# Cross-attention and a routed feed-forward layer on one core: VectorE's LayerNorm and routing steps put at the end of each group of heads

## The chip, the cores and the metric

The kernel runs on one core of one Trainium2 chip. The metric is the device time of one execution in microseconds (us). Five engines work side by side, each through its own list of instructions in order: TensorE (PE, matmuls), VectorE (DVE), ScalarE (ACT), GpSimd (POOL) and SyncE (SP, which issues DMAs). They meet at semaphores only.

## The reference

```python
x = x + xattn(layernorm(x), ctx, Wq, Wk, Wv, Wo, bo)     # x: 16 x 256 x 128, ctx: 16 x 1601 x 96, 16 heads of 64
x = x + ffn(layernorm(x), router_weight, ...)             # 32 experts, 4 groups of 8, top 2 groups, top 4 experts
...
def _route(tokens, router_weight, router_bias):
    scores = sigmoid(tokens @ router_weight.T)
    sfc = scores + router_bias
    group_scores = top_k(sfc.reshape(T, 4, 8), 2)[0].sum(-1)
    gmask = the 2 best groups of 4
    topk_idx = top_k(where(gmask > 0, sfc, 0), 4)
    topk_w = scores[topk_idx]; topk_w = topk_w / (topk_w.sum(-1) + 1e-20) * 2.5
```

## The kernel before, in words

All 16 batches are worked through one after the other. A batch has 256 queries and 1601 keys, its 16 heads go in four groups of four heads, so there are 64 groups, called here by their number i = 0 to 3 in the batch. The loop on each engine covers two batches (`par` 0 and 1) a turn, eight turns in all.

In a group the 1601 keys go in 13 steps s = 0 to 12 of up to 128 keys (the last has 65). A step is: TensorE makes the scores in PSUM (`scores`, 6 matmuls of 512 columns, since each fp32 product is made from a high and a low fp32r half); ScalarE takes the exponential twice (`exp`), once as fp32 `p_full`, once as its high half `p_hi`; the low half `p_lo` = `p_full` - `p_hi` is a subtraction over 128 x 1024, made by GpSimd for steps 3, 5, 7 and 9 (`POOL_STEPS`) and by VectorE for the nine others (`lo(s)`, L1004); TensorE then weighs the values (`weigh`, 6 matmuls), two steps behind the scores.

Between these, TensorE does side jobs, whose results land in two banks of PSUM (`side`), used in turn, and which VectorE has to empty: TensorE waits in `side_jobs` until the job before the last has been emptied (`s_drain`). The table `PLACES` says which jobs stand at which step t, and all engines go through it in the same order. M jobs (32 a group) make scores for the next group's maxima, and VectorE takes the maximum (L1016); Y jobs project finished heads and VectorE adds them to the tokens `x1`; T turns the maxima; the two Q jobs at step 12 project queries of a later group. L turns normalised tokens for the attention of the next batch, N turns those of a finished batch for the feed-forward part, R makes router logits.

VectorE also has steps that are no jobs. LayerNorm is `token_stats` (means and variances, ending in `var_eps`), a power -0.5 on GpSimd (`deviations`), and `normalise` (`xn`). Routing is a chain of small dependent instructions on 128 x 64 values and less. Before, the function `between` puts these inside the group, by step t: the statistics after `lo(6)` at t = 7 of groups i = 0 and 1, `normalise` at t = 3 of groups 1 and 2, and in group 3 the routing in four parts at t = 6, 7, 8 and 10.

GpSimd, besides its four `p_lo` a group, splits a quarter of the next batch's context into halves at each group (`split_piece`, four instructions, L368 to L373). After the 64 groups comes the feed-forward part: 8 chunks of 512 tokens, 17 pairs of experts (the first the shared one) in each, and there VectorE also routes the last tokens in the second chunk.

Of the kernel before, what the change touches and what calls it, by code (L numbers as in the profile page):

```python
# [11 lines left out]
P = 128  # L12
# [6 lines left out]
def xattn_moe(nc, x, ctx_keys, ctx_turned, attn_w, bo, router_wT, router_b, moe_w, out):  # L19
# [29 lines left out]
    with stack:  # L49
# [9 lines left out]
        w_all = sb(stack, "w_all", [P, T + 2, 2 * E])  # L59
# [7 lines left out]
        power = sb(stack, "power", [P, 2])  # L67
        stats = sb(stack, "stats", [P, 2, 6])
        moments = sb(stack, "moments", [P, 2, 2])
        var_eps = sb(stack, "var_eps", [P, 2])  # L70
        rstd = sb(stack, "rstd", [P, 2])
        xn = sb(stack, "xn", [P, 2, D])
# [126 lines left out]
        PLACES = {2: ("MM", "M"), 3: ("MM", "M"), 4: ("MM", "MM"), 5: ("MM", "MX"), 6: ("MM", "MM"),  # L199
                  7: ("MM", "MM"), 8: ("MM", "MY"), 9: ("MM", "MM"), 10: ("MM", "MM"), 11: ("YY", "YT"),  # L200
                  12: ("", "QQ")}
        EXTRA = ("", "L", "N", "R")
        KINDS = "MLNRYTQ"

        def places(i):
            return {t: tuple(part.replace("X", EXTRA[i]) for part in ab) for t, ab in PLACES.items()}

# [91 lines left out]
        def _(pool):  # L299
# [7 lines left out]
            def deviations(count):  # L307
                pool.wait_ge(s_var, count)
                pool.tensor_tensor(rstd[:, :], var_eps[:, :], power[:, :], ALU.pow).then_inc(s_rstd, 1)
# [12 lines left out]
            deviations(1)  # L322
# [3 lines left out]
            pool.memset(v_lo[:, :, :, DC:OW].bitcast(F32), 0.0)  # L326
            pool.memset(choice[:, :, E:E + TOP_K], -BIG)
# [30 lines left out]
            def split_piece(bb, par, i):  # L358
# [10 lines left out]
                pool.tensor_copy(v_hi[:, other, tiles, 0:DC], keys_nat[:, tiles, :]).then_inc(s_sh, 1)  # L369
                pool.wait_ge(s_sh, bb * (2 * NGB) + (g + 2))  # L370
# [5 lines left out]
            with pool.Fori(0, B // 2) as bb:  # L376
                for par in range(2):
                    for i in range(NGB):
                        g = group_of(par, i)
                        split_piece(bb, par, i)  # L380
# [4 lines left out]
                        if i < 2:  # L385
                            deviations(bb * 4 + (2 * par + 2 + i))

            deviations(2 * B + 2)
# [19 lines left out]
        def _(pe):  # L408
# [3 lines left out]
            def turn_tokens(where, count):  # L412
                pe.wait_ge(s_xn, count)
                for t in range(2):
                    mm = pe.transpose(where[:, t * P:(t + 1) * P], xn[:, t, :], ident[:, :])
                mm.then_inc(s_fill, 1)
# [38 lines left out]
            turn_tokens(bank(J0_X), 1)  # L455
# [73 lines left out]
            def body(bb, par, i):  # L529
# [7 lines left out]
                def side_jobs(kinds):  # L537
                    for kind in kinds:
# [5 lines left out]
                        if kind == "M":  # L544
                            if k == 0:
                                pe.wait_ge(s_qh, bb * (4 * NGB) + (2 * g + 4))
                            if i == NGB - 1 and k in (0, 3 * NM // 4):
                                pe.wait_ge(s_v, bb * (2 * NGB) + (par * NGB + (2 * NGB - 1 if k == 0 else 2 * NGB)))
                            max_scores(where, k, (i + 1) % 2, next_par).then_inc(s_fill, 1)
                        elif kind == "L":  # L550
                            turn_tokens(where, bb * 4 + (2 * par + 2))
                        elif kind == "N":
                            turn_tokens(where, bb * 4 + (2 * par + 3))
# [28 lines left out]
                pe.wait_ge(s_ex, n + S)  # L582
                scores(0, (i + 1) % 2, next_par)
# [21 lines left out]
            turn_tokens(bank(JOBS_END + GH), 2 * B + 2)  # L605
# [10 lines left out]
            def turn_routing(c):  # L616
                for t in range(4):
                    mm = pe.transpose(op[0:2 * E, 1, t * P:(t + 1) * P], w_all[:, 2 + c * 4 + t, :], ident[:, :])
                mm.then_inc(s_wf, 1)
# [18 lines left out]
            for c in range(NCH):  # L638
                for q in range(NP):
# [25 lines left out]
                    if q == 10 and c + 1 < NCH:  # L665
                        if c:
                            pe.wait_ge(s_fin, c)
                        if c + 1 == NCH - 1:
                            pe.wait_ge(s_rw, B + 1)
# [6 lines left out]
        def _(act):  # L676
# [52 lines left out]
            def body(bb, par, i):  # L729
# [20 lines left out]
                for s in range(1, S):  # L750
                    exp(s)
                    if s == 5 and EXTRA[i]:
                        j = job_at[i][EXTRA[i]][0]
                        where, filled = bank(jobs0 + j), jobs + (j + 1)
                        if EXTRA[i] == "L":
                            tokens_hi(where, 1 - par, filled)
                        elif EXTRA[i] == "N":
# [76 lines left out]
        def _(dve):  # L834
# [11 lines left out]
            def token_stats(tiles, base=0):  # L846
                for q in range(2):
                    ins = dve.bn_stats(stats[:, q, :], x1[:, tiles[q], :])
                link(ins, base)
                carry()  # L850
                for q in range(2):
                    ins = dve.bn_aggr(moments[:, q, :], stats[:, q, :])
                link(ins, base)
                dve.tensor_scalar(var_eps[:, :], moments[:, :, 1], EPS, None, ALU.add).then_inc(s_var, 1)

            def normalise(tiles, count):
                dve.wait_ge(s_rstd, count)
                for q in range(2):
                    ins = dve.tensor_scalar(xn[:, q, :], x1[:, tiles[q], :], moments[:, q, 0:1], rstd[:, q:q + 1],  # L859
# [39 lines left out]
            def add_one(count):  # L899
                dve.wait_ge(s_ls, count)  # L900
                dve.tensor_scalar(ra[:, :, :], ex[:, :, :], 1.0, None, ALU.add).then_inc(s_drain, 1)

            def route_scores(drained, base=0):
                dve.wait_ge(s_drain, drained)
# [8 lines left out]
                link(ins, base)  # L913

            def route_groups(base=0):
                flat = g_sum[:, :, :].rearrange("p t g -> p (t g)")
                link(dve.tensor_tensor(flat, top8[:, :, 0], top8[:, :, 1], ALU.add), base)  # L917
# [9 lines left out]

            def route_experts(base=0):
                for t in range(2):
                    kept = choice[:, t, 0:E].rearrange("p (g e) -> p g e", g=N_EGROUP)  # L930
                    keep = g_keep[:, t, :].rearrange("p (g a) -> p g a", a=1).to_broadcast([P, N_EGROUP, E // N_EGROUP])
                    ins = dve.tensor_tensor(kept, kept, keep, ALU.mult)
                link(ins, base)
# [3 lines left out]
                link(ins, base)  # L937
                carry()
# [6 lines left out]

# [224 lines left out]
```

## Time and profile before

| | us |
|---|---|
| median of 3 runs (lowest to highest) | 3604.51 (3602.98 to 3604.76) |
| the profiled execution | 3602.96 |
| its span, first to last instruction | 3600.8 |
| 64 groups, from the first output kept to the last | 43.1 to 3263.8 |
| TensorE busy | 3386.3 (94%) |
| VectorE busy | 2578.8 (72%) |
| ScalarE busy | 1935.5 (54%) |
| GpSimd busy | 1076.8 (30%) |
| mean granted clock of TensorE | 0.975 of full |

Each engine's share is of the span. The records of matmuls overlap: each lasts longer than the distance to the next one, so an engine may be called busy and still not be at its fastest. The row on idle time, in square brackets behind an instruction, tells how long its engine had done nothing and whose result ended that.

### The profile page before, as it was taken

The numbers are of one execution on the slowest core, as the hardware profiler recorded it, in microseconds if no ns is written. First come the engines' busy times: TensorE is split into PE (matmuls) and PEld (weight loads), VectorE is DVE, ScalarE is ACT, GpSimd is POOL, SyncE is SP. The second block draws the span as 40 slices with busy tenths as digits, with TensorE's granted clock in tenths as the row PEclk, the third lists the DMA queues.
The fourth block names the chain that finished last, engine by engine and source line by source line (L and its number), as shares of the span: only waits on it lengthen the run. The fifth ranks groups of instructions, "written<-read, shape, count | busy, mean of one in ns | idle before, by whom it ended". The sixth has DMA issues, their size and how long they took to land.

```text
span 3600.8 us, 50491 instructions
## 1 busy us (share of the span) xinstructions
PE 3386.3 (94%) x15589; PEld 2655.2 (74%) x15589; DVE 2578.8 (72%) x4960; ACT 1935.5 (54%) x2239; POOL 1076.8 (30%) x737
## 2 busy tenths in 40 slices
PE   7999999999999999999999999999999999999999
PEld 6777777777777777777777777777777777777887
DVE  6777777777777777777777777777777777776655
ACT  4555555555555555555555555555555555555554
POOL 4222232222222222222222222222232222324555
PEclk9999999999999999999999999999999999999999
DMA  2000000000000000000000000000000000000000
GB/s 84 1 15 1 16 1 15 1 15 2 2 14 1 16 1 15 1 15 2 15 1 1 16 1 15 1 15 2 15 1 1 16 1 15 1 15 27 9 7 9
DMA packets 8682, 35.98 MB, mean 10 GB/s; under 512 B 1657, under 2 KB 2306, under 8 KB 8130
## 3 DMA queue, kind: packets, MB, share of 16 engines
q1 hardware_dynamic: 8386, 32.29, 2.9%
q8 instruction: 154, 2.52, 0.3%
q14 instruction: 142, 1.16, 0.1%
HBM read 29.92 MB, written 2.10 MB: 9 GB/s over the span
## 4 chain that ended last, share of the span: by engine, by line
PE 77%; DVE 11%; issue 9%; POOL 1%; DVEq 0%; ACT 0%; POOLq 0%; DMA 0%; ACTq 0%
PE side L449 10%; PE op L513 9%; PE op L516 9%; PE st L499 9%; PE op L519 9%; PE st L502 9%; PE st L505 9%; PE side L525 3%; DVE m_part L1016 3%; DVE p_lo L1004 3%; PE st L614 2%; PE st L612 2%; PE st L613 2%; DVE xn L859 1%; DVE g_sum L917 1%
## 5 line engine op out<-in xcount | busy, mean ns | idle before, releaser
L742 ACT ACTIVATE p_full<-st 128x1024 f32<-128x1024 f32 (+1 forms) x832 | 855.0, 1028 | 1457.2 <-PE st L505 1457.2
L1016 DVE TENSOR_REDUCE m_part<-side 128x1 f32<-128x402 f32 x2048 | 1096.7, 571 | 529.9 <-PE side L449 520.6
L383 POOL TENSOR_TENSOR p_lo<-p_full,p_hi 128x1024 fp32r<-128x1024 f32 x256 | 649.1, 2536 | 2096.8 <-ACT p_hi L745 2096.8
L1004 DVE TENSOR_TENSOR p_lo<-p_full,p_hi 128x1024 fp32r<-128x1024 f32 (+1 forms) x576 | 709.0, 1231 | 266.3 <-ACT p_hi L745 266.3
L745 ACT ACTIVATE p_hi<-st 128x1024 fp32r<-128x1024 f32 (+1 forms) x832 | 850.6, 1022 | 0.0
L449 PE MATMUL side<-cT_hi,qT_hi 96*128 96x402 f32 x2048 | 613.1, 364 | 178.5 <-DVE m_part L1016 165.0
L449 PEld LDWEIGHTS side<-cT_hi,qT_hi 96*128 96x128 f32 x2048 | 395.0, 193 | 344.6 <-DVE m_part L1016 220.2
L499 PE MATMUL st<-qT_hi,cT_hi 97*128 97x512 f32 (+1 forms) x1668 | 548.3, 410 | 3.2 <-DMA qT_hi<-m_row 3.0
L513 PE MATMUL op<-p_hi,v_hi 128*97 128x512 f32 (+1 forms) x1664 | 540.4, 407 | 0.0
L516 PE MATMUL op<-p_lo,v_hi 128*97 128x512 f32 (+1 forms) x1664 | 533.0, 402 | 0.0
L519 PE MATMUL op<-p_hi,v_lo 128*97 128x512 f32 (+1 forms) x1664 | 532.3, 402 | 0.0
L502 PE MATMUL st<-qT_lo,cT_hi 96*128 96x512 f32 (+1 forms) x1668 | 529.5, 398 | 0.0
L505 PE MATMUL st<-qT_hi,cT_lo 96*128 96x512 f32 (+1 forms) x1668 | 523.4, 395 | 0.0
L502 PEld LDWEIGHTS st<-qT_lo,cT_hi 96*128 96x128 f32 (+1 forms) x1668 | 312.9, 188 | 82.9
L505 PEld LDWEIGHTS st<-qT_hi,cT_lo 96*128 96x128 f32 (+1 forms) x1668 | 306.8, 184 | 83.8
L516 PEld LDWEIGHTS op<-p_lo,v_hi 128*97 128x97 f32 (+1 forms) x1664 | 277.4, 167 | 120.2
L519 PEld LDWEIGHTS op<-p_hi,v_lo 128*97 128x97 f32 (+1 forms) x1664 | 277.4, 167 | 119.7
L499 PEld LDWEIGHTS st<-qT_hi,cT_hi 97*128 97x128 f32 (+1 forms) x1668 | 301.2, 189 | 32.5 <-issue 3.7
L513 PEld LDWEIGHTS op<-p_hi,v_hi 128*97 128x97 f32 (+1 forms) x1664 | 273.3, 168 | 30.9
L402 POOL TENSOR_TENSOR h_lo<-hid,h_hi 128x512 fp32r<-128x512 f32 x136 | 176.2, 1295 | 137.1 <-ACT h_hi L807 137.0
L525 PEld LDWEIGHTS side<-B_all,oT 97*128 97x128 f32 x1040 | 153.7, 200 | 28.8 <-DVE m_part L1016 12.2
L892 DVE SCALAR_TENSOR_TENSOR x<-side,recip,x 128x128 f32 (+1 forms) x520 | 158.5, 347 | 11.1 <-DVE recip L889 2.5
(142 smaller groups left out, 2760.9 us busy)
## 6 DMA issues: line engine op xcount, KB each, us to landing
keys_nat<-in_ctx_keys SPq DMA_DIRECT2D x18, 624.0 KB, 5.8
keys_tur<-in_ctx_turned SPq DMA_DIRECT2D x18, 603.0 KB, 5.0
out_x<-x SPq DMA_DIRECT2D x8, 256.0 KB, 2.0
x<-in_x SPq DMA_DIRECT2D x1, 1920.0 KB, 12.8
w_rest<-in_moe_w SPq DMA_DIRECT2D x1, 1152.0 KB, 6.8
qT_hi<-m_row SPq DMA_DIRECT2D x65, 4.0 KB
w_first<-in_moe_w SPq DMA_DIRECT2D x1, 960.0 KB, 5.0
aw<-in_attn_w SPq DMA_DIRECT2D x2, 448.0 KB, 6.1
```

The costliest lines, as they stand in the source:

```text
L383: pool.tensor_tensor(p_lo[:, slot(s), :], p_full[:, s % 2, :], p_hi[:, slot(s), :].bitcast(F32), ALU.subtract).then_inc(s_lo_pool, 1)
L449: return pe.matmul(where[:, 0:MAXW], qT_hi[0:DC, slot, tile * P:(tile + 1) * P], cT_hi[0:DC, par, part * MAXW:(part + 1) * MAXW], start=Tr ...
L499: pe.matmul(st[0:m, s % 2, j, :], cT_hi[:, par, keys], qT_hi[:, slot, halves[j]], start=True, stop=False)
L502: pe.matmul(st[0:m, s % 2, j, :], cT_hi[0:DC, par, keys], qT_lo[:, slot, halves[j]], start=False, stop=False)
L505: mm = pe.matmul(st[0:m, s % 2, j, :], cT_lo[:, par, keys], qT_hi[0:DC, slot, halves[j]], start=False, stop=True)
L513: pe.matmul(op[0:OW, j, :], v_hi[0:m, par, s, :], p_hi[0:m, slot(s), halves[j]], start=(s == 0), stop=False)
L516: pe.matmul(op[0:OW, j, :], v_hi[0:m, par, s, :], p_lo[0:m, slot(s), halves[j]], start=False, stop=False)
L519: mm = pe.matmul(op[0:OW, j, :], v_lo[0:m, par, s, :], p_hi[0:m, slot(s), halves[j]], start=False, stop=(s == S - 1))
L742: act.activation(p_full[0:m, s % 2, :], both(st[0:m, s % 2]), ACT.Exp, scale=SCALE)
L745: act.activation(p_hi[0:m, slot(s), :], both(st[0:m, s % 2]), ACT.Exp, scale=SCALE).then_inc(s_ex, 1)
L1004: dve.tensor_tensor(p_lo[0:m, slot(s), :], p_full[0:m, s % 2, :], p_hi[0:m, slot(s), :].bitcast(F32), ALU.subtract).then_inc(s_lo, 1)
L1016: dve.tensor_reduce(m_part[:, at:at + 1], where[:, 0:MAXW], AX.X, ALU.max).then_inc(s_drain, 1)
```

## The change

The function `between` is taken out, and a function `after_jobs` is called behind the last side job of the group instead. The statistics of all four tiles of tokens (two for the next batch, two finished) are taken in one go at the end of group 0; `normalise` for all four and the middle part of the routing stand at the end of group 1; the last part of the routing at the end of group 2; its first part at the end of group 3. L moves from group 1 to group 2 and N one step on, to t = 6. In group 3 the R job's bank is now given free by a memset (`exponentials_seen`), and the addition of one goes with the first part of the routing. The small tiles of LayerNorm double, so that four tiles fit. On GpSimd one power instruction over four columns at step 3 of group 1 takes the place of two over two columns, at the ends of groups 0 and 1.

```diff
-                def between(t):
...
-                    if i == 0 and t == 7:
-                        token_stats([dve.snap(bb * 4 + (2 * par + 4 + q)) for q in range(2)], links)
-                    elif i == 1 and t == 3:
-                        normalise([dve.snap(bb * 4 + (2 * par + 4 + q)) for q in range(2)], bb * 4 + (2 * par + 2))
...
-                    elif i == 3 and t == 6:
-                        route_scores(jobs + (job_at[i]["R"][0] + 1), links)
-                    elif i == 3 and t == 7:
+                def after_jobs():
...
+                    if i in (0, 1):
+                        tiles = [dve.snap(bb * 4 + (2 * par + q)) for q in (4, 5, 0, 1)]
+                    if i == 0:
+                        dve.wait_ge(s_drain, jobs + (job_at[i]["Y"][-1] + 1))
+                        token_stats(tiles, 0, links)
+                    elif i == 1:
+                        normalise(tiles, 0, bb * 2 + (par + 2))
                         route_groups(links)
...
+                    elif i == 2:
                         route_weights(bass.ds(bb * 4 + 2 * par, 2), links)
+                    else:
+                        route_scores(links)
...
-                    between(t)
                     side_jobs(at[t][1])
-
...
+                after_jobs()
...
-        EXTRA = ("", "L", "N", "R")
+        EXTRA = {2: {5: "L", 6: "N"}, 3: {5: "R"}}
...
-            def split_piece(bb, par, i):
+            def piece_hi(bb, par, i):
...
+            def piece_lo(bb, par, i):
...
-                        split_piece(bb, par, i)
+                        piece_hi(bb, par, i)
+                        piece_lo(bb, par, i)
...
-                        if i < 2:
-                            deviations(bb * 4 + (2 * par + 2 + i))
-
+                            if s == 3 and i == 1:
+                                deviations(bb * 2 + (par + 2), slice(0, 4))
...
                     if c == 1:
-                        if q == 8:
-                            route_scores(JOBS_END + GH + 2)
+                        if q == 5:
+                            route_groups()
+                        elif q == 8:
+                            route_weights(slice(T, T + 2))
                         elif q == 10:
+                            route_scores()
+                        elif q == 12:
                             route_groups()
-                        elif q == 12:
-                            route_experts()
                         elif q == 14:
-                            route_weights(slice(T, T + 2))
+                            route_weights(slice(T + 2, T + 4))
```

TensorE's wait for the context before the maxima of the next batch now counts the high half only (`s_sh`), and a wait for all of it (`s_v`) stands ahead of the first scores of that batch.

VectorE's order before, in group 3 at steps t = 6 and 7; `m_part` rows are M jobs, and each of them gives TensorE a bank back:

```order
L1016 TENSOR_REDUCE m_part<-side 128x1
L1003 REGISTER_ALU
L1004 TENSOR_TENSOR p_lo<-p_full,p_hi 128x1024
L917 TENSOR_TENSOR g_sum<-top8 128x8
L840 REGISTER_ALU
L920 TENSOR_TENSOR g_more<-g_sum 128x32
L921 TENSOR_TENSOR g_same<-g_sum 128x32
L840 REGISTER_ALU
L923 TENSOR_TENSOR g_same<-g_same,earlier 128x32
```

VectorE's order in the changed kernel, from the last side jobs of group 1 (the two `qT_lo`) on into group 2:

```order
L888 TENSOR_TENSOR qT_lo<-side,qT_hi 96x512
L870 ISA
L872 TENSOR_SCALAR xn<-x1,moments,rstd 128x128 x4
L933 TENSOR_TENSOR g_more<-g_sum 128x32
L934 TENSOR_TENSOR g_same<-g_sum 128x32
L852 REGISTER_ALU
L936 TENSOR_TENSOR g_same<-g_same,earlier 128x32
L852 REGISTER_ALU
L937 TENSOR_TENSOR g_more<-g_more,g_same 128x32
```

The comparison of groups (`g_more`, `g_same`) stood behind a `p_lo` and ahead of M jobs in the middle of group 3; now it stands between the last Q job of group 1 and the `p_lo` of step 0 of group 2, together with four `xn`.

GpSimd's order in the changed kernel, where group 0 ends and group 1 goes to its step 3:

```order
L392 TENSOR_TENSOR p_lo<-p_full,p_hi 128x1024
L371 CAST cT_hi<-keys_tur 96x402
L372 CAST v_hi<-keys_nat 128x4x96
L378 REGISTER_ALU
L379 TENSOR_TENSOR cT_lo<-keys_tur,cT_hi 96x402
L381 TENSOR_TENSOR v_lo<-keys_nat,v_hi 128x4x96
L391 REGISTER_ALU
L392 TENSOR_TENSOR p_lo<-p_full,p_hi 128x1024
L308 ISA
L309 TENSOR_TENSOR rstd<-var_eps,power 128x4
```

The four instructions of the split stand as before behind the last `p_lo` of one group and ahead of the first `p_lo` of the next; only the power instruction has moved.

## Rows read from the trace of the kernel before

**Rows 1.** The page: busy time and share of each engine; the chain by engine.
```profile
PE 3386.3 (94%) x15589; PEld 2655.2 (74%) x15589; DVE 2578.8 (72%) x4960; ACT 1935.5 (54%) x2239; POOL 1076.8 (30%) x737
...
PE 77%; DVE 11%; issue 9%; POOL 1%; DVEq 0%; ACT 0%; POOLq 0%; DMA 0%; ACTq 0%
```

**Rows 2.** One line, L727 (one a group): count, ns min/median/max, first and last start.
```profile
L727 ACT ACTIVATE oT<-op x65: 1024/1028/1028, 43.1 to 3263.8; 97x1024 f32<-97x1024 f32 x65
```

**Rows 3.** Stretches, groups i = 0 to 3 of one batch: length, busy us (instructions), PEclk, DMA.
```profile
1049.03:1097.22 48.19, 46.28 (x218) 36.14 (x217) 34.62 (x63) 27.08 (x31) 16.90 (x14) 1.00 0.00 1
1097.22:1148.72 51.50, 47.83 (x220) 37.33 (x219) 36.73 (x66) 27.47 (x32) 13.62 (x9) 0.97 0.00 1
1148.72:1196.74 48.02, 46.02 (x220) 36.35 (x219) 34.57 (x60) 27.47 (x31) 12.99 (x8) 1.00 0.09 27
1196.74:1250.82 54.08, 50.03 (x224) 38.72 (x223) 40.70 (x97) 27.32 (x31) 10.12 (x4) 0.94 0.01 2
```

**Rows 4.** TensorE in order of time: start, us, instruction, count, idle before.
```profile
1106.04 0.35 PE L449 MATMUL side<-cT_hi,qT_hi 96*128 96x402 f32 x1
1108.38 0.45 PE L449 MATMUL side<-cT_hi,qT_hi 96*128 96x402 f32 x1 [2.00 <-DVE m_part L1016]
...
1120.68 0.53 PE L449 MATMUL side<-cT_hi,qT_hi 96*128 96x402 f32 x2
...
1124.29 1.19 PE L449 MATMUL side<-cT_hi,qT_hi 96*128 96x402 f32 x2 [1.67 <-DVE m_part L1016]
...
1224.27 1.19 PE L449 MATMUL side<-cT_hi,qT_hi 96*128 96x402 f32 x2 [2.95 <-DVE m_part L1016]
```

**Rows 5.** VectorE in order of time, the `normalise` of group 1.
```profile
1105.19 2.65 DVE L859 TENSOR_SCALAR xn<-x,moments,rstd 128x128 f32 x2
```

**Rows 6.** GpSimd in order of time, its first `p_lo` of the same group.
```profile
1104.99 2.51 POOL L383 TENSOR_TENSOR p_lo<-p_full,p_hi 128x1024 fp32r<-128x1024 f32 x1 [18.31 <-ACT p_hi L745]
```

**Rows 7.** Four lines of VectorE: count, ns min/median/max, first and last start.
```profile
L859 DVE TENSOR_SCALAR xn<-x,moments,rstd x68: 334/1616/2880, 5.3 to 3271.2; 128x128 f32 x64, 128x128 f32<-128x128 f32 x4
...
L854 DVE TENSOR_SCALAR var_eps<-moments x34: 169/1537/1544, 3.8 to 3269.9; 128x2 f32<-128x2 f32 x34
...
L917 DVE TENSOR_TENSOR g_sum<-top x17: 433/2349/2354, 213.1 to 3340.2; 128x8 f32<-128x8 f32 x17
...
L901 DVE TENSOR_SCALAR ra<-ex x17: 195/1881/1890, 205.1 to 3275.6; 128x64 f32<-128x64 f32 x17
```

**Rows 8.** Stretches at the lower clock, in groups 1 and 3 of that batch.
```profile
1124.20:1127.60 3.40, 3.31 (x8) 2.34 (x9) 1.58 (x4) 0.47 (x1) 0.00 (x0) 0.50 0.00 0
...
1223.20:1230.00 6.80, 5.73 (x16) 4.46 (x17) 4.67 (x22) 0.17 (x1) 0.00 (x0) 0.50 0.00 0
```

**Rows 9.** VectorE in order of time, where group 1 ends and group 2 begins.
```profile
1144.41 1.28 DVE L875 TENSOR_TENSOR qT_lo<-side,qT_hi 96x512 fp32r<-96x512 f32 x2
1148.87 1.23 DVE L1004 TENSOR_TENSOR p_lo<-p_full,p_hi 128x1024 fp32r<-128x1024 f32 x1 [3.18 <-ACT p_hi L745]
```

**Rows 10.** TensorE in order of time, the first values weighed in group 2.
```profile
1151.20 0.63 PE L513 MATMUL op<-p_hi,v_hi 128*97 128x512 f32 x2
```

**Rows 11.** VectorE in order of time: statistics, middle of the routing, end of the routing.
```profile
1121.42 0.48 DVE L848 BATCH_NORM_STATS2 stats<-x 128x6 f32 x2
...
1222.34 0.19 DVE L920 TENSOR_TENSOR g_more<-g_sum 128x32 f32<-128x32 f32 x1
...
1223.63 1.06 DVE L1016 TENSOR_REDUCE m_part<-side 128x1 f32<-128x402 f32 x2
...
1235.77 0.21 DVE L947 TENSOR_TENSOR ra<-struck,choice 128x64 f32<-128x64 f32 x1
...
1237.66 0.23 DVE L956 TENSOR_TENSOR w_all<-ra,w_all 128x64 f32 x1
```

**Rows 12.** Stretches of 39.5 us in the feed-forward part: the third chunk, the second.
```profile
3372.73:3412.27 39.54, 39.54 (x179) 32.54 (x178) 23.43 (x36) 20.61 (x38) 23.29 (x19) 1.00 0.02 8
3333.20:3372.70 39.50, 38.01 (x169) 30.55 (x168) 30.78 (x71) 19.39 (x34) 22.14 (x18) 1.00 0.01 2
```

More of the change, by code:

```diff
@@ L66, in xattn_moe @@
         earlier = sb(stack, "earlier", [P, N_EGROUP, N_EGROUP])
[L67 to L72, printed above, removed]
+        power = sb(stack, "power", [P, 4])
+        stats = sb(stack, "stats", [P, 4, 6])
+        moments = sb(stack, "moments", [P, 4, 2])
+        var_eps = sb(stack, "var_eps", [P, 4])
+        rstd = sb(stack, "rstd", [P, 4])
+        xn = sb(stack, "xn", [P, 4, D])
         x2f = sb(stack, "x2f", [P, 2 * P])
@@ L305, in link, with deviations @@
                 pool.wait_ge(s_plink, steps[0])
-            def deviations(count):
+            def deviations(count, which):
                 pool.wait_ge(s_var, count)
-                pool.tensor_tensor(rstd[:, :], var_eps[:, :], power[:, :], ALU.pow).then_inc(s_rstd, 1)
+                pool.tensor_tensor(rstd[:, which], var_eps[:, which], power[:, which], ALU.pow).then_inc(s_rstd, 1)
             link(pool.memset(ident[:, :], 0.0))
@@ L326, in _ @@
             pool.memset(v_lo[:, :, :, DC:OW].bitcast(F32), 0.0)
+            pool.memset(sigmoid[:, :, :], 0.0)
+            pool.memset(g_sum[:, :, :], 0.0)
+            pool.memset(choice[:, :, 0:E], 0.0)
             pool.memset(choice[:, :, E:E + TOP_K], -BIG)
@@ L369, in split_piece @@
                 pool.tensor_copy(v_hi[:, other, tiles, 0:DC], keys_nat[:, tiles, :]).then_inc(s_sh, 1)
+            def piece_lo(bb, par, i):
+                g, other = group_of(par, i), 1 - par
+                cols = slice(i * MAXW, (i + 1) * MAXW)
+                tiles = slice(PIECES[i], PIECES[i] + 4)
                 pool.wait_ge(s_sh, bb * (2 * NGB) + (g + 2))
@@ L582, in body @@
                 pe.wait_ge(s_ex, n + S)
+                if i == NGB - 1:
+                    pe.wait_ge(s_v, bb * (2 * NGB) + (par * NGB + 2 * NGB))
                 scores(0, (i + 1) % 2, next_par)
@@ L844, in carry, with token_stats, normalise @@
                 dve.memset(spare[:, :], 0.0)
-            def token_stats(tiles, base=0):
-                for q in range(2):
-                    ins = dve.bn_stats(stats[:, q, :], x1[:, tiles[q], :])
+            def token_stats(tiles, first, base=0):
+                for q, tile in enumerate(tiles):
+                    ins = dve.bn_stats(stats[:, first + q, :], x1[:, tile, :])
                 link(ins, base)
                 carry()
-                for q in range(2):
-                    ins = dve.bn_aggr(moments[:, q, :], stats[:, q, :])
+                for q in range(len(tiles)):
+                    ins = dve.bn_aggr(moments[:, first + q, :], stats[:, first + q, :])
                 link(ins, base)
-                dve.tensor_scalar(var_eps[:, :], moments[:, :, 1], EPS, None, ALU.add).then_inc(s_var, 1)
-            def normalise(tiles, count):
+                which = slice(first, first + len(tiles))
+                dve.tensor_scalar(var_eps[:, which], moments[:, which, 1], EPS, None, ALU.add).then_inc(s_var, 1)
+            def normalise(tiles, first, count):
                 dve.wait_ge(s_rstd, count)
-                for q in range(2):
-                    ins = dve.tensor_scalar(xn[:, q, :], x1[:, tiles[q], :], moments[:, q, 0:1], rstd[:, q:q + 1],
+                for q, tile in enumerate(tiles, first):
+                    ins = dve.tensor_scalar(xn[:, q, :], x1[:, tile, :], moments[:, q, 0:1], rstd[:, q:q + 1],
                                             ALU.subtract, ALU.mult)
@@ L926, in route_groups @@
                 link(dve.tensor_scalar(g_keep[:, :, :], g_keep[:, :, :], TOPK_EGROUP - 0.5, None, ALU.is_lt), base)
[L928 to L933, printed above, removed]
+                kept = choice[:, :, 0:E].rearrange("p t (g e) -> p t g e", g=N_EGROUP)
+                keep = g_keep[:, :, :].rearrange("p t (g a) -> p t g a", a=1)
+                link(dve.tensor_tensor(kept, kept, keep.to_broadcast([P, 2, N_EGROUP, E // N_EGROUP]), ALU.mult), base)
                 carry()
@@ L937, in route_experts, with route_weights @@
                 link(ins, base)
+            def route_weights(tiles, base=0):
                 carry()
@@ L944, in route_experts @@
                 link(ins, base)
-            def route_weights(tiles, base=0):
                 link(dve.tensor_tensor(ra[:, :, :], struck[:, :, 0:E], choice[:, :, 0:E], ALU.not_equal), base)
```

68 lines of the change are left out of this document (31 added, 37 removed).

## The prediction

> **What bounds the kernel now.** I read the page first: TensorE is busy for 94% of the span, and the chain that ended last lies on it for 77%, but also for 11% on VectorE and for 9% on "issue" [rows 1]. So there are places where TensorE stands and VectorE is late. To find them I cut the span into the 64 groups. The copy of the output (L727) runs once a group, 65 times from 43.1 to 3263.8 us, which is 50.32 us a group, 201.3 us a batch [rows 2]. The view by stretches then shows that the four groups of a batch are unlike: 48.19, 51.50, 48.02 and 54.08 us, though TensorE has nearly the same work (218, 220, 220, 224 matmuls in the records). The two long ones also have a lower mean clock, 0.97 and 0.94 [rows 3].
>
> TensorE in order of time shows the stalls. In group 1 an M job starts at 1106.04 and the next at 1108.38, where two M jobs that meet no wait start 0.18 us apart (0.53 for a pair of 0.35 each). That is 2.16 us lost, and what ended it was VectorE's maximum. It happens again at 1124.29, and in group 3 at 1224.27 with 2.95 us of idle time [rows 4]. The maxima are late because of what stands ahead of them on VectorE: the two `xn` at 1105.19 took 2.65 us together [rows 5]. One `xn` takes 0.334 us at its quickest, 1.616 in the median; `var_eps`, on two columns, 0.169 and 1.537; `g_sum`, on eight columns, 0.433 and 2.349; the addition of one, 0.195 and 1.881 [rows 7]. A duration that doesn't go with the size is a wait inside the instruction. GpSimd's `p_lo` ran from 1104.99 for 2.51 us, to 1107.50 [rows 5, 6], and the first `xn` began 0.2 us after it and the pair was over 0.34 us after it: VectorE was held until GpSimd was done. The Trainium skill, GPSIMD Engine Reference, "Key points", says that GpSimd shares its SBUF interfaces with VectorE and contends with instructions of two SBUF inputs or in a mode that uses both ports; the trace agrees for these four, and the M jobs' maxima, read from PSUM, come right behind without such a wait.
>
> The clock is the second part. It is at 0.50 for 3.4 us behind the second stall of group 1 and for 6.8 us behind the long one of group 3 [rows 8]. Both times it fell while or just after TensorE stood; in the third chunk of the feed-forward part TensorE is busy for all of 39.54 us and the clock is at 1.00 [rows 12].
>
> **The change, part by part.**
>
> *Stalls removed.* With no LayerNorm or routing step ahead of M jobs, the stalls go. Group 0 loses that of `var_eps`, group 1 those of `xn` and `var_eps`, group 2 that of `xn`: each 2.16 to 2.3 us with the late restart, I take 2.2, so 4 x 2.2 = 8.8 us a batch. Group 3 loses the long one, 2.95 us idle plus 0.17 (a record is 0.35 long and the next could start 0.18 after it) plus a slow pair (1.19 for 0.53, of which half is the clock): 3.4 us. The added one costs VectorE 1.881 - 0.195 = 1.7 us more than it need; what reaches TensorE lies between 0 and 1.7, I take 1.0. The chain of `route_weights` took 2.12 us from 1235.77 to 1237.89 [rows 11] ahead of M jobs; between 0 and 2.1 reaches TensorE, I take 0.5 as an estimate. Sum 13.7 us a batch.
>
> *Clock.* In the two slow stretches TensorE was busy for 3.31 and 5.73 us [rows 8]; at full clock the same work takes half, so 1.65 + 2.85 = 4.5 us a batch. By the Trainium skill, TensorE: Matmul & The Clock Gate, "Terms", the penalty is about the throttled time by one less the ratio of clocks; from the 10.2 us that would be 5.1 us, and the forecast 10 us lower. I stay with the busy time, as part of the slow stretch was idle anyway.
>
> *Cross-check.* 13.7 + 4.5 = 18.2 us a batch. The other way: group 2 has one stall and no clock loss, 48.02 - 2.2 = 45.8; group 0 gives 48.19 - 2.2 = 46.0 [rows 3]. Four such groups are 183.4, against 201.3: 17.9 us. I take 18.1, and 16 batches give 290 us. VectorE is then busy for about 33 us of 45.8, so it does not become the bound.
>
> *What is put at the ends.* Between the last Q job (VectorE done at 1145.69) and the `p_lo` of the next group's step 0 (1148.87, it waits for the exponential) VectorE is idle for 3.18 us. That `p_lo` is over at 1150.10 and TensorE first needs it at 1151.20 [rows 9, 10], so a further 1.1 us of lateness costs nothing: a cover of 4.28 us. Prices without the hold: the pair of statistics is 0.48 us [rows 11], the aggregates I estimate at no more, `var_eps` at 0.17 [rows 7], so 1.1 for two tiles and up to 2.1 us for four. End of group 1: four `xn` at up to 0.334, 1.3 us, the comparisons from 1222.34 to 1223.63, 1.3 us [rows 7, 11], and the selection, three instructions estimated at 0.2 each like the small rows: 3.0 to 3.3 us. End of group 2: five more of that kind, overlapping, 0.6 (an estimate), and the 2.12 of the weights: 2.7. End of group 3: addition, reciprocal, bias, eight small maxima and a sum, by the same 0.2 each with the maxima overlapping about 2.2, at most 3 (an estimate too). All lie below 4.28, three at or below 3.0. They are cheap there only if GpSimd is idle; ahead of its first `p_lo` in group 1 it had been idle for 18.31 us [rows 6], that is since 1086.68, over the whole end of group 0 (1097.22). I take 0 for the four ends; bounds 0 and 1 us each.
>
> *L and N in one group, the power on GpSimd, TensorE's waits.* L is no longer in group 1, and stands with N in group 2: the same matmuls. `xn` is ready a whole group earlier than it is read. One GpSimd power instruction a batch goes. The wait for `s_v` is long met. Cost 0, cover: several steps of 3.5 us. The split on GpSimd is not moved at all (its order shows it), so that part of the change is nothing.
>
> *Feed-forward part.* In the second chunk VectorE routes twice instead of once, beside a GpSimd that works all the time, so holds come back. Before, this chunk's stretch had 1.5 us of TensorE idle in 39.50 [rows 12]. VectorE was busy there for 30.78 us against 23.43, so the routing took 7.4 us of busy time; it takes nearly twice that now, in bigger pieces. Between +1 and +9 us, I take +5.
>
> *Sum.* Against the profiled execution's span: 3600.8 - 290 + 5 = 3315.8. The median of the runs lies 3.7 above the span (3604.51): 3319.5 us, 7.9% less.
>
> **Rivals.**
>
> *The clock falls as before.* If the low clock had another cause than the stalls, 4.5 x 16 = 72 us stay: 3391 us. For it: stalls in groups 0 and 2 are followed by no drop, both have a mean clock of 1.00 [rows 3]. Against it: both drops come right behind a stall [rows 4, 8], and the unbroken chunk has none [rows 12]. Chance 7%.
>
> *The ends spill, or new stalls take part of the gain.* The small steps have waits of a few hundredths each that could be longer after a register instruction, or N's and L's copies hold a bank in group 2. At 0.5 to 1 us an end that is 32 to 64 us: 3350 to 3383 us. For it: group 1's end fills the idle time. Against: the further 1.1 us. Chance 13%.
>
> *Slower than before.* GpSimd works at the group ends after all, and every held instruction there waits for it: place, the end of each group ahead of `p_lo` of step 0; price 2.2 us for each held one. With four an end, 8.8 + 2.4 - 4.28 = 6.9 us are lost at each, 27.6 a batch against 18.1 won: 3604 + 152 = 3756 us. It decides once the ends take 8.8 us on the mean. Against it is the 18.31 us of idle time. Chance 3%.
>
> *The gain is not there* (M jobs wait for something else right behind, and the groups stay near 50 us): 3590 to 3610 us. Against: group 2 has 2.0 us without a matmul in all, which is its one stall [rows 3, 4]. Chance 2%.
>
> **The numbers.** 75% for the forecast with its own range, 3303 to 3345. The range must leave out no more than 2 in 10: from 3303 to 3375 it takes in most of the spill. A difference of 0.2%, 7 us, is about what a measurement of this kernel can tell. Faster by more than that 0.95, within it 0.02, slower 0.03.
>
> **What the profile after would show.** Right: all four groups of a batch 45.5 to 46.2 us long, clock 1.00 from group 0 to 63, `xn`, `var_eps`, `ra` and `g_sum` in the loop at their shortest durations, VectorE's idle time ahead of `p_lo` of step 0 down from 3.18 to 0.1 to 1.6 us, TensorE's waits for `m_part` near nothing, the second feed-forward chunk some us longer. Wrong: low clock still once or twice a batch, long small instructions at the ends, TensorE waiting ahead of the first `op` matmuls of a group, or groups that differ by over 1 us.

## The result, and the profile after

| | before | after |
|---|---|---|
| median of the runs, us | 3603.94 (3602.98 to 3604.76) | 3340.26 (3337.08 to 3342.82) |
| the profiled execution, span | 3600.8 | 3335.1 |
| 64 groups, first output kept to the last | 43.1 to 3263.8 | 41.3 to 2992.7 |
| mean granted clock | 0.975 | 0.996 |

The ratio is 0.9268 with a 95% interval of 0.9252 to 0.9284: 264 us, or 7.3%, less, where 285 were forecast (3319 us). In the spans the 64 groups went from 3220.7 to 2951.4 us, 269.3 less, the part behind them from 337.0 to 342.4, 5.4 more, and the part ahead from 43.1 to 41.3. This last part took between 41.2 and 47.1 us in the twelve profiles of this case, and not by kernel (the changed one had 41.3 and 41.2, a variant that differs only behind it 45.8). So a difference of up to 5 us between two medians need not come from the groups, and for small differences the time of the 64 groups is the better measure: the changed kernel's two profiles have 2951.4 and 2952.2 us.

The page of the changed kernel, busy time and the chain that ended last:

```profile
PE 3285.0 (98%) x15589; PEld 2611.9 (78%) x15589; DVE 2414.3 (72%) x4954; ACT 1937.9 (58%) x2239; POOL 1073.8 (32%) x724
...
PE 89%; issue 6%; DVE 3%; POOL 2%; ACT 0%; DMA 0%; DVEq 0%; POOLq 0%; ACTq 0%
```

VectorE's share of the chain fell from 11% to 3% [rows 1], and its busy time by 164 us, though it does nearly the same work (4954 instructions for 4960): that was time held inside instructions. Four groups of one batch of the changed kernel by stretches, as in [rows 3], and below them group 0 of another batch, the third:

```profile
965.25:1011.23 45.98, 45.75 (x219) 36.16 (x218) 33.80 (x67) 27.10 (x31) 16.35 (x13) 1.00 0.00 1
1011.23:1056.70 45.47, 45.47 (x219) 36.24 (x218) 34.15 (x71) 27.10 (x30) 14.00 (x9) 1.00 0.01 1
1056.70:1103.35 46.65, 46.16 (x223) 36.54 (x222) 34.56 (x75) 27.88 (x33) 13.03 (x8) 1.00 0.10 28
1103.35:1149.36 46.01, 46.01 (x223) 36.72 (x222) 33.42 (x71) 27.33 (x32) 10.14 (x4) 1.00 0.01 2
409.32:458.44 49.12, 47.26 (x219) 37.16 (x218) 33.80 (x67) 27.22 (x30) 17.03 (x13) 0.97 0.01 2
```

The groups are nearly alike now, close to the length worked out, but for two things to explain: group 2 is 0.6 to 1.2 us longer than the others, and one group 0 took 49.12 us with the clock at 0.97. The small instructions of VectorE, lines as in [rows 7]:

```profile
L872 DVE TENSOR_SCALAR xn<-x,moments,rstd x68: 330/337/2879, 5.4 to 3000.1; 128x128 f32 x64, 128x128 f32<-128x128 f32 x4
...
L867 DVE TENSOR_SCALAR var_eps<-moments x18: 169/170/493, 4.0 to 2998.8; 128x4 f32<-128x4 f32 x16, 128x2 f32<-128x2 f32 x2
...
L928 DVE TENSOR_TENSOR g_sum<-top x17: 171/172/484, 223.9 to 3075.3; 128x8 f32<-128x8 f32 x17
...
L917 DVE TENSOR_SCALAR ra<-ex x17: 178/181/856, 222.1 to 3072.4; 128x64 f32<-128x64 f32 x17
```

Their medians are at the shortest value: 0.337 for 1.616 us, 0.170 for 1.537, 0.172 for 2.349, 0.181 for 1.881. VectorE in order of time over the end of group 1, the place of [rows 9]:

```profile
1052.38 1.28 DVE L888 TENSOR_TENSOR qT_lo<-side,qT_hi 96x512 fp32r<-96x512 f32 x2
1053.58 1.10 DVE L872 TENSOR_SCALAR xn<-x,moments,rstd 128x128 f32 x4
1054.60 0.18 DVE L933 TENSOR_TENSOR g_more<-g_sum 128x32 f32<-128x32 f32 x1
...
1056.17 0.18 DVE L945 MAX8 best<-choice 128x8 f32<-128x32 f32 x1
1056.84 1.23 DVE L1013 TENSOR_TENSOR p_lo<-p_full,p_hi 128x1024 fp32r<-128x1024 f32 x1 [0.49 <-ACT p_hi L756]
```

The work there takes from 1053.66 to 1056.35, 2.7 us, and leaves 0.49 us idle ahead of a `p_lo` that starts 0.14 us after the group's begin, as before.

Two waits of TensorE are new in the changed kernel's list of waits (who waited for whom, us in total, times, longest):

```profile
PE side L424 <- DVE m_part L1025: 7.8, 16, 0.5
...
PE op L522 <- DVE p_lo L1013: 6.8, 7, 1.9
...
PE side L458 <- DVE m_part L1025: 1.7, 8, 0.2
```

The last is the wait that stood at 165 us in the kernel before. The first is N in group 2, once a batch; the second comes ahead of the first values weighed, seven times, that is once for each turn of the loop but the first. The chain of the changed kernel in order of time at one of them (start, us, what; L1070 is VectorE's loop):

```profile
408.02 0.18 DVE g_sum L928
408.20 0.03 issue
408.23 0.04 DVEq L1070
408.27 0.03 issue
408.30 0.06 DVEq L1070
408.36 3.23 issue
411.59 0.06 DVEq L1070
411.65 0.05 issue
411.70 2.05 DVE p_lo L1013
413.75 0.04 issue
413.79 0.71 PE op L522 x2
```

Routing ends, VectorE's loop branches, and 3.23 us pass in which it waits for nothing that the profile shows. Then `p_lo` of step 0 starts 2.38 us late against the group's begin, where 0.14 is usual, and is held by GpSimd's split on top (2.03 for 1.23 us). GpSimd's last two instructions of that split are these:

```profile
411.61 1.04 POOL L379 TENSOR_TENSOR cT_lo<-keys_tur,cT_hi 96x402 fp32r<-96x402 f32 x1
412.61 1.93 POOL L381 TENSOR_TENSOR v_lo<-keys_nat,v_hi 128x384 fp32r<-128x384 f32 x1
```

The two engines take turns. `p_lo` starts while `cT_lo` runs, and needs 0.8 us more than it takes alone; `cT_lo` is over at 412.65. `v_lo` then stands behind `p_lo` and needs 1.0 us more than the 0.93 that it takes alone. TensorE waited 1.86 us here, and its clock fell for 3.4 us right behind. At the six other turns `p_lo` came 2.1 to 2.2 us behind the group's begin, TensorE waited 0.8 to 0.9 us, the clock stayed, and the group took 46.7 to 46.8 us.

In the kernel before such a turn lay inside the 3.2 to 3.7 us of idle time at a group's end, and no `p_lo` of step 0 in the loop was late. The Trainium skill, Runtime: NRT & Kernel Launch, "Instruction fetch mechanics", says that a taken branch to a page out of the current window forces a fetch by DMA before execution goes on; the trace has packets of the instruction queues from 407 to 412.5 us, 6 of them, and none in mid-turn from 961 to 966. The packets are not told apart by engine, and the other engines come round their loops too, so that VectorE's 3.23 us are this fetch is not shown. That they belong to the loop's turn is shown by the runs below.

### The profile page after: what moved, and what is told of

Same layout as the page of the kernel before. It is cut to its first block, busy times and chain, and to the rows that moved or that the text cites. A ratio compares the mean times of both kernels' runs of the same rounds, so it can differ in the third digit from the quotient of the medians.

```text
span 3335.1 us, 50432 instructions
## 1 busy us (share of the span) xinstructions
PE 3285.0 (98%) x15589; PEld 2611.9 (78%) x15589; DVE 2414.3 (72%) x4954; ACT 1937.9 (58%) x2239; POOL 1073.8 (32%) x724
## 4 chain that ended last, share of the span: by engine, by line
PE 89%; issue 6%; DVE 3%; POOL 2%; ACT 0%; DMA 0%; DVEq 0%; POOLq 0%; ACTq 0%
PE st L511 11%; PE st L508 11%; PE op L522 11%; PE st L514 11%; PE op L525 10%; PE side L458 10%; PE op L528 10%; PE side L534 3%; PE st L623 2%; PE st L625 2%; PE st L624 2%; POOL p_lo L392 1%; PE op L623 1%; PE op L625 1%; PE op L624 1%
## 5 line engine op out<-in xcount | busy, mean ns | idle before, releaser
L458 PE MATMUL side<-cT_hi,qT_hi 96*128 96x402 f32 x2048 | 567.0, 347 | 1.8 <-DVE m_part L1025 1.7
L508 PE MATMUL st<-qT_hi,cT_hi 97*128 97x512 f32 (+1 forms) x1668 | 540.5, 405 | 2.9 <-DMA qT_hi<-m_row 2.9
L522 PE MATMUL op<-p_hi,v_hi 128*97 128x512 f32 (+1 forms) x1664 | 527.5, 398 | 6.8 <-DVE p_lo L1013 6.8
L525 PE MATMUL op<-p_lo,v_hi 128*97 128x512 f32 (+1 forms) x1664 | 519.8, 393 | 0.0
L528 PE MATMUL op<-p_hi,v_lo 128*97 128x512 f32 (+1 forms) x1664 | 519.6, 393 | 0.0
L458 PEld LDWEIGHTS side<-cT_hi,qT_hi 96*128 96x128 f32 x2048 | 385.2, 188 | 120.8 <-DVE m_part L1025 7.5
L525 PEld LDWEIGHTS op<-p_lo,v_hi 128*97 128x97 f32 (+1 forms) x1664 | 269.8, 162 | 115.6
L528 PEld LDWEIGHTS op<-p_hi,v_lo 128*97 128x97 f32 (+1 forms) x1664 | 270.0, 162 | 115.1 <-issue 0.2
L522 PEld LDWEIGHTS op<-p_hi,v_hi 128*97 128x97 f32 (+1 forms) x1664 | 265.2, 164 | 38.6 <-DVE p_lo L1013 9.1
L1116 DVE TENSOR_TENSOR gu_mul<-st,act_g 128x512 f32<-128x512 f32 x128 | 88.4, 691 | 102.8 <-PE side L670 95.7
```

Of the source, the lines that this page charges most:

```text
L458: return pe.matmul(where[:, 0:MAXW], qT_hi[0:DC, slot, tile * P:(tile + 1) * P], cT_hi[0:DC, par, part * MAXW:(part + 1) * MAXW], start=Tr ...
L508: pe.matmul(st[0:m, s % 2, j, :], cT_hi[:, par, keys], qT_hi[:, slot, halves[j]], start=True, stop=False)
L522: pe.matmul(op[0:OW, j, :], v_hi[0:m, par, s, :], p_hi[0:m, slot(s), halves[j]], start=(s == 0), stop=False)
L525: pe.matmul(op[0:OW, j, :], v_hi[0:m, par, s, :], p_lo[0:m, slot(s), halves[j]], start=False, stop=False)
L528: mm = pe.matmul(op[0:OW, j, :], v_lo[0:m, par, s, :], p_hi[0:m, slot(s), halves[j]], start=False, stop=(s == S - 1))
```

## The experiments

The kernel before ran beside each of them. Its median was 3606.7 us beside the first four, 3608.26 beside the next four and 3606.12 beside the last two. A line "..." in an edit stands for lines left out.

**LayerNorm half a step later, in the kernel before.**

```diff
-                    if i == 0 and t == 7:
+                    if i == 0 and t == 8:
...
-                    elif i == 1 and t == 3:
+                    elif i == 1 and t == 4:
...
-                    elif i == 1 and t == 7:
+                    elif i == 1 and t == 8:
...
-                    elif i == 2 and t == 3:
+                    elif i == 2 and t == 4:
```

> The kernel before, with only its LayerNorm steps half a step later: the statistics of groups 0 and 1 at t = 8 instead of 7, the two normalise of groups 1 and 2 at t = 4 instead of 3. The same VectorE instructions still stand ahead of M jobs in the middle of the group, but where GpSimd is between two of its p_lo. Theory of the hold (the stalls come from VectorE waiting inside an instruction for GpSimd): each of the four stalls of 2.2 us shrinks to under 0.7, and with the second stall of group 1 its clock loss of 1.65 us goes: 4 x 1.5 to 2.2 and 1.65 are 8 to 10 us a batch, so 3604 - 128 to 160 = 3444 to 3476 us. Rival (any VectorE work ahead of M jobs in mid-group stalls TensorE, whatever GpSimd does): the same stalls at another place, 3595 to 3610 us.

Measured: 3436.33 us, ratio 0.9531 (0.9516 to 0.9546), 170 us less, more than either theory had written down. The 64 groups took 3056.0 us for 3220.7. Its groups of one batch, and two of its lines:

```profile
995.20:1041.16 45.96, 45.76 (x218) 36.15 (x217) 33.18 (x63) 27.09 (x31) 16.91 (x14) 1.00 0.00 1
1041.16:1086.92 45.76, 45.76 (x220) 36.42 (x219) 33.25 (x66) 27.47 (x31) 13.68 (x9) 1.00 0.00 1
1086.92:1132.65 45.73, 45.73 (x221) 36.42 (x220) 32.51 (x60) 27.48 (x32) 13.01 (x8) 1.00 0.10 28
1132.65:1186.78 54.13, 50.09 (x224) 38.77 (x223) 40.70 (x97) 27.31 (x31) 10.12 (x4) 0.94 0.01 2
```

```profile
L859 DVE TENSOR_SCALAR xn<-x,moments,rstd x68: 336/341/2879, 5.3 to 3104.7; 128x128 f32 x64, 128x128 f32<-128x128 f32 x4
...
L854 DVE TENSOR_SCALAR var_eps<-moments x34: 169/169/172, 3.7 to 3103.3; 128x2 f32<-128x2 f32 x34
```

The same instructions, still in mid-group and ahead of M jobs, cost TensorE nothing once they don't meet GpSimd's `p_lo`: groups 0 to 2 stand at 45.7 to 46.0 us. For LayerNorm the hold is shown, and the rival on the amount of work falls. Of the 264 us of the change, about 170 are the meeting of LayerNorm and GpSimd. The rest is group 3, which is untouched here: 54.13 against 46.0 us, less the new costs below. There the rows show the same pattern (`g_sum` 2.349 us in the median before, 0.172 after). But no run moved the routing within group 3 alone, so how much of this part was the hold, and how much the work in that place, is argued and not shown.

**N as the second side job of its place.**

```diff
-        EXTRA = {2: {5: "L", 6: "N"}, 3: {5: "R"}}
+        EXTRA = {2: {3: "N", 5: "L"}, 3: {5: "R"}}
```

> The changed kernel with N of group 2 at t = 3 instead of t = 6, so that it is the second side job in its place and not the third. Theory: the 0.9 us by which group 2's step at N is longer (4.45 against 3.53 us) come from three side jobs on two banks in a row, TensorE waits 0.49 us for the first to be emptied; at t = 3 the wait and its restart go, only N's two transposes (0.2 us) stay: 0.7 us a batch, 11 us, ratio to the changed kernel 0.9967, about 3329 us. Rival (N costs its time wherever it stands, through ScalarE's copy ahead of an exponential): no change, 3340 us.

Measured: 3328.92 us, 11.3 less than the changed kernel's 3340.26; ratio to before 0.9232 (0.9219 to 0.9245). In the profile the wait of N for `m_part` is gone, and group 2 has 45.9 us for 46.65, which is 0.7 us a batch and 11.5 in all. The theory of three jobs on two banks holds.

**Which turn's routing is late.** In these two the condition was written the wrong way round: the kernel labelled as leaving the routing out of the first batch leaves it out of the second, and the other way about. Each expectation belongs to the other's kernel; they are quoted as they stand.

```diff
-                    else:
+                    elif par == 0:
                         route_scores(links)
...
```

> The changed kernel without route_scores at the end of group 3 of the first of the two batches of a loop turn (half of the tokens get wrong routing, the work left out is about 2.2 us of VectorE per turn). Theory of the loop's turn (VectorE needs 3.5 us to come round its loop, and route_scores ahead of it makes the first p_lo late; in mid-turn nothing is late): no change against the changed kernel, 3340 us. Rival (the end of group 3 is too full wherever it stands): 3 to 5 us less.

This kernel keeps the routing at the end of the first batch, in mid-turn, and has none ahead of the branch. Its five runs took 3326.4 to 3332.66 us, the median is 3326.61, ratio 0.9229 (0.9217 to 0.9242), 13.6 less than the changed kernel. The expectation that belongs to it, the one below, had 8 to 9; by the groups of the profile it is 8.6.

> The changed kernel without route_scores at the end of group 3 of the second batch of a loop turn, the one ahead of the branch (half of the tokens get wrong routing). Theory of the loop's turn: 7 turns lose 0.8 us each less, and the one with 2.0 us and a clock drop (3.1 us) too: 8 to 9 us less than the changed kernel, 3331 us. Rival (the end of group 3 is too full wherever it stands): 3 to 5 us less, as without the one of the first batch.

With `elif par == 1:` the routing stays ahead of the branch and is left out in mid-turn. Measured: 3336.73 us, ratio 0.9254 (0.9242 to 0.9267), 3.5 less. The expectation that belongs to it is the one above: no change by the theory, 3 to 5 us less by the rival. So by its time alone this kernel did what the rival said. VectorE in order of time at the same loop top, first of the one without routing ahead of the branch, then of the one with it:

```profile
782.19 1.23 DVE L1013 TENSOR_TENSOR p_lo<-p_full,p_hi 128x1024 fp32r<-128x1024 f32 x1 [3.18 <-ACT p_hi L756]
```

```profile
780.55 0.17 DVE L928 TENSOR_TENSOR g_sum<-top 128x8 f32<-128x8 f32 x1
783.72 1.48 DVE L1013 TENSOR_TENSOR p_lo<-p_full,p_hi 128x1024 fp32r<-128x1024 f32 x1 [3.00 <-issue]
```

In the first the next `p_lo` waits for the exponential, in the second for the branch, 3.00 us. In the profiles the 64 groups took 2942.8 us without routing ahead of the branch and 2947.3 without it in mid-turn, against 2951.4. The first is 8.6 us less, as the theory has it. The second is 4.1 less, and its groups tell where: after a turn group 0 still takes 46.5 to 46.7 us, and in mid-turn `p_lo` of step 0 is as punctual as in the changed kernel, with the routing and without it. What went is the one fall of the clock (49.1 us down to 46.5, 2.6 us), and three of the mid-turn `p_lo` of step 1 missed GpSimd's split (45.5 for 46.0 us, 1.5 together). So the end of group 3 was not too full in mid-turn, and the theory stands.

**The changed kernel again**, as the base of the three that follow.

> The changed kernel again, unedited, as the base of the three others of this call: 3337 to 3343 us.

Measured: 3340.95 us (3337.62 to 3346.33), ratio 0.9264 (0.9251 to 0.9277). Its groups ran from 41.2 to 2993.4, 2952.2 us.

**The first part of the routing at the end of group 0**, behind the statistics. The last batch's part stands behind the loop.

```diff
...
                     if i == 0:
...
                         token_stats(tiles, 0, links)
+                        route_scores(links)
...
-                    else:
-                        route_scores(links)
...
             steps[0] = head_steps + B // 2 * links_per_turn
+            route_scores()
```

> The changed kernel with route_scores at the end of group 0, behind the statistics, instead of the end of group 3; nothing is left out. Theory of the loop's turn (VectorE needs 3.2 to 3.4 us to come round its loop, 2.1 us of routing ahead of the branch make the first p_lo of a turn late): the seven loop tops lose their 0.8 us and the one its 3.1, and the end of group 0, 1.6 and 2.1 us, stays under the cover of 4.28: 9 to 13 us less than the changed kernel, ratio 0.997. Rival (the cost goes with the amount of work at an end, and group 0's end is now the fullest): 16 ends are late instead of 7 or 8, 5 to 15 us more.

Measured: 3332.03 us, 8.9 less than its base; ratio 0.9233 (0.9220 to 0.9246). In the loop TensorE waits for no `p_lo` any more, and the clock stays up. VectorE in order of time over this fullest end:

```profile
1006.61 1.28 DVE L888 TENSOR_TENSOR qT_lo<-side,qT_hi 96x512 fp32r<-96x512 f32 x2
1007.81 0.86 DVE L860 BATCH_NORM_STATS2 stats<-x 128x6 f32 x4
...
1011.09 0.18 DVE L928 TENSOR_TENSOR g_sum<-top 128x8 f32<-128x8 f32 x1
1011.39 1.23 DVE L1013 TENSOR_TENSOR p_lo<-p_full,p_hi 128x1024 fp32r<-128x1024 f32 x1
```

3.4 us of work from 1007.89 to 1011.27 put `p_lo` 0.46 us behind the group's begin for the usual 0.14, and nothing follows from it. The lateness that costs nothing was read as 1.1 us from [rows 9, 10], and the loop's turns of the changed kernel bear it out: there `p_lo` was 2.0 us later than usual and TensorE waited 0.8.

**Both edits together.**

> Both edits, route_scores at the end of group 0 and N at t = 3. If the two costs are apart, they add: 11 us for N and 9 to 13 for the loop's turn, 3340 - 22 = 3318 us, ratio to the changed kernel 0.993 to 0.994. If they hide one another, about 3328.

Measured: 3321.41 us (3316.57 to 3322.39), ratio 0.9204 (0.9192 to 0.9217), 19.5 less than the base. Alone the two edits gave 8.9 and 11.3, 20.2 together, so the two costs add. The 64 groups take 2931.2 us, 45.8 each.

**And GpSimd's split in group 0 behind its `p_lo` of steps 3 and 5.**

```diff
-                        piece_hi(bb, par, i)
-                        piece_lo(bb, par, i)
+                        if i:
+                            piece_hi(bb, par, i)
+                            piece_lo(bb, par, i)
...
+                            if i == 0 and s == 3:
+                                piece_hi(bb, par, i)
+                            if i == 0 and s == 5:
+                                piece_lo(bb, par, i)
```

> The kernel with both edits, and in group 0 GpSimd splits its quarter of the context behind its p_lo of steps 3 (high halves) and 5 (low halves), not at the start of the group. Theory of the hold: the p_lo of step 1 on VectorE, held there to 2.0 us instead of 1.22, is free, and group 0's 0.5 us at its second pair of M jobs go; the high halves (1 us) fit between two of VectorE's p_lo, the low ones (1.9 us) may hold the p_lo of step 6 by up to 1 us, which has more slack than the one of step 1: 4 to 8 us less, about 3311. Rival (the hold only moves): 3315 to 3322, as without the edit.

Measured: 3314.82 us (3310.16 to 3315.5), ratio to before 0.9184 (0.9171 to 0.9196), 6.6 less than without the edit, and all its runs lie below all of those. The profiles' groups went from 2931.2 to 2923.9 us. The `p_lo` of step 1 in group 0, first without and then with the edit:

```profile
961.05 2.01 DVE L1013 TENSOR_TENSOR p_lo<-p_full,p_hi 128x1024 fp32r<-128x1024 f32 x1
```

```profile
964.09 1.21 DVE L1018 TENSOR_TENSOR p_lo<-p_full,p_hi 128x1024 fp32r<-128x1024 f32 x1
```

Over all 576 `p_lo` of VectorE the longest is 1.227 us now, where it was 1.996 in the kernel before. So the hold did not move to another `p_lo`, as the rival had it. This is the best version found, 26 us under the changed kernel.

**A stall put back, without routing or LayerNorm.**

```diff
+                    if i == 1 and t in (7,):
+                        for _ in range(5):
+                            link(dve.memset(xn[:, :, :], 0.0), links)
...
```

> The changed kernel with five extra memsets of 128 x 512 in a row on VectorE (no routing, no LayerNorm, and not held by GpSimd in the kernel before) ahead of M jobs at t = 7 of group 1, about 2.2 us if one takes 0.4 us. Theory of the clock (it falls where TensorE stands too long, not at a place of the program): one stall of about 2 us a batch, 16 x 2 = 32 us; stalls of this size had no drop behind them in groups 0 and 2 before, so the clock stays at 1.00 in most batches: 3365 to 3385 us. Rival (the place in group 1 makes the drop): also 16 drops of 1.6 us, 3400 us.

Measured: 3419.52 us, ratio 0.9480 (0.9464 to 0.9496): 79 us over the changed kernel, more than either theory. A memset took 0.485 us for the 0.4 assumed, so the idle time was 2.81 us and not 2.2, and the clock fell behind 14 of the 16 stalls. The theory had expected it to stay up in most batches; that was wrong for a stall of this size, and of 2.2 us nothing is measured. Two of its groups 1 by stretches, with and without a drop:

```profile
1039.77:1090.07 50.30, 47.49 (x219) 37.21 (x218) 36.75 (x76) 27.10 (x31) 13.96 (x9) 0.97 0.00 1
1608.01:1656.86 48.85, 46.01 (x219) 36.20 (x218) 36.65 (x76) 27.10 (x31) 13.94 (x9) 1.00 0.00 1
```

The stall by itself costs 48.85 - 45.49 = 3.4 us, a drop of 3.4 us about 1.5 more (1.2 to 1.6 in seven groups), one of 6.8 us 2.4 to 2.7 (in seven). With `t in (3, 7)`:

> The same with five memsets at t = 3 and five at t = 7 of group 1, the two places at which TensorE stood in the kernel before. Theory of the clock: two stalls of about 2 us, 64 us, and with them the low clock behind the second returns as it was in the kernel before, 1.6 us a batch, 26 us: 3420 to 3440 us. Rival (the low clock came from something else that the change took away): twice the cost of one stall and no drop, 3400 us.

Measured: 3490.05 us, ratio 0.9679 (0.9663 to 0.9695), 150 us over the changed kernel, again more than either had it, the stalls being longer than planned. TensorE in order of time behind the first of the two:

```profile
1067.23 0.35 PE L458 MATMUL side<-cT_hi,qT_hi 96*128 96x402 f32 x1
1070.40 0.45 PE L458 MATMUL side<-cT_hi,qT_hi 96*128 96x402 f32 x1 [2.82 <-DVE m_part L1025]
1070.68 0.63 PE L522 MATMUL op<-p_hi,v_hi 128*97 128x512 f32 x2
1071.15 0.99 PE L525 MATMUL op<-p_lo,v_hi 128*97 128x512 f32 x2
1071.93 1.06 PE L528 MATMUL op<-p_hi,v_lo 128*97 128x512 f32 x2
```

A pair of matmuls goes from 0.63 to 1.06 us: the clock fell here, at t = 3, where it never fell in the kernel before with 2.0 us of idle time [rows 4]. The profile has 26 drops in 32 stalls, two in most of the groups. With the drop at a loop's turn in group 0 that makes three places. So in the 64 groups the low clock goes with TensorE's standing and not with one place in the program; without a stall there is none. What is not settled is which stall suffices: 1.67 us had a drop behind it in every group 1 before and none in group 0.

## Why the prediction was right, point by point

**Stalls removed, 13.7 us a batch, and clock, 4.5.** The mechanism is shown by the first experiment for LayerNorm, and its size by the groups. LayerNorm's part of the sum was 8.8 and 1.65, 10.45 us a batch; the first experiment took 10.3 off. Group 3's part was 3.4, 1.0, 0.5 and 2.85, 7.75 us; between that experiment and the kernel with both places mended lie 7.8. The two guesses in it, 1.0 for the addition of one and 0.5 for the weights, were not measured apart. Together it is 18.1 us a batch, as forecast, and 16.8 in the changed kernel, which has the two costs below. The cross-check in the prediction has a slip: its four groups add up to 183.6 and not 183.4 us, which makes the mean 18.0 and the forecast 2 us higher.

The clock's part is right in size: a 3.4 us drop cost about 1.5 us in the experiment with one stall, 1.65 in the sum, and a 6.8 us one 2.4 to 2.7 for 2.85. All 32 drops in the loop are gone, and one came at a new place. The rival of a clock that falls as before is refuted.

**L and N, cost 0.** This was wrong. "The same matmuls" was true, but N became the third side job in a row at t = 6, and two banks let only two be made ahead. It cost 0.7 us a batch, 11 us in all (3340.26 to 3328.92). It could have been read from `PLACES` and the rule on `s_drain`. The spill rival had named a bank held in group 2, though by the copies and not by the order of the jobs.

**The four ends, cost 0.** Right in three of them: the work was 2.7 us at the end of group 1, where 3.0 to 3.3 had been worked out, and even 3.4 us at an end cost nothing. Wrong at the end of group 3 for every second batch, where the branch of VectorE's loop follows: I took 3.18 us to be idle time, but the turn took 3.0 to 3.5 us by itself. That cost 8.9 us, with one drop of the clock in it. Without these two the kernel measures 3321.41 us, and the forecast was 3319. So nearly all of the miss lies in these two terms, which the sum had at 0, and the rest of it held.

**The two rules of the Trainium skill.** That GpSimd and VectorE share SBUF interfaces (GPSIMD Engine Reference, "Key points") was borne out by the first experiment and by the split. The section on the chip says that the engines meet at semaphores only; by these runs, VectorE and GpSimd also meet at SBUF. The rule on the penalty of the clock (TensorE: Matmul & The Clock Gate, "Terms") would have put the forecast 10 us lower, and was the worse of the two sums: a 3.4 us drop cost about 1.5 us and not 1.7, a 6.8 us one 2.4 to 2.7 and not 3.4.

**GpSimd's split, no change.** Its order did not change and it held the `p_lo` of step 1 as before. Moved for real, it gave 6.6 us.

**Feed-forward part, +5.** It measured 5.4 in the spans. The figure was a choice within +1 to +9, so that it came so close is in part luck.

**What the profile was to show.** Groups of 45.5 to 46.2 us (all but group 2 and the group 0 behind a turn), short small instructions and next to no waits for `m_part` came as said; the things that were named as signs of the spill (TensorE waiting ahead of the first `op` matmuls, groups that differ) came too, in small.

## What to carry to other kernels

When tiny instructions take 1.5 to 2.4 us in a profile, look at what GpSimd does in that time before counting their work: shifting them by half a step out of its long instruction was worth 170 us here, without moving any work away. Idle time at the end of a stage is only free if nothing invisible lies in it; at a loop's branch 3 us of it are the turn itself, and the mid-loop stages do not show that. Where jobs go round two banks, count how many stand in a row ahead of a consumer that is behind, and put a new one where it makes two, not three.

## What the runs showed of the hardware

- VectorE adding, subtracting or scaling from SBUF to SBUF waits inside the instruction until a subtraction of GpSimd's is done: up to 2.35 us for 8 columns. Beside the same GpSimd instructions `bn_stats` and `bn_aggr` took at most 0.03 us more, and memsets, `max`, `match_replace` and what was read from PSUM no more than alone (the maxima of M jobs: 0.57 us either way). GpSimd is held too: its `v_lo` took 1.93 us beside a `p_lo` of VectorE and 0.93 alone.
- VectorE's way round its loop took 3.0 to 3.5 us from its last instruction to its next, which the kernel before hid in the idle time at a group's end.
- TensorE's clock went to its lower level (0.50 of full) behind single idle times of 2.8 us in 14 cases of 16, and in 13 of 16 at another place of the group, for 3.4 or 6.8 us, at a cost of 1.2 to 2.7 us each. At a loop's turn it fell all four times that TensorE had stood 1.85 to 1.86 us (in three profiles), and never behind 1.0 us or less; but behind 2.0 us in groups 1 and 2 of the kernel before it never did.
